# A gate whose bias is added by TensorE and whose logits are copied by ScalarE, in a language-model tower with attention and a mixture of experts

## What is computed

```
logits = jnp.einsum('btd,de->bte', x, Wg) + bg
gates = jax.nn.softmax(logits, axis=-1)
vals, idx = jax.lax.top_k(gates, TOP_K)
vals = vals / (jnp.sum(vals, axis=-1, keepdims=True) + EPS)
```

## Time and profile before

| | us |
|---|---|
| median of 3 runs | 352.75 |
| lowest and highest run | 352.64 and 353.0 |
| the profiled execution, its own time | 354.0 |
| its span, first to last instruction | 352.2 |
| mean granted TensorE clock | 0.973 |

### The profile page before, as it was taken

The page is one execution under the profiler, slowest core; times in us unless marked ns, Lnnn a source line. Parts: engine busy times, 40 slices in busy tenths (PEclk is TensorE's granted clock), DMA queues, the critical chain, the costliest instruction groups (busy, mean ns, idle before and its releaser), DMA issues.

```text
span 352.2 us, 11441 instructions
## 1 busy us (share of the span) xinstructions
PE 325.4 (92%) x3017; PEld 289.2 (82%) x3017; DVE 302.1 (86%) x1190; ACT 255.4 (73%) x754; POOL 197.3 (56%) x346
## 2 busy tenths in 40 slices
PE   8947999999999999999978699999998999999983
PEld 3615888888878787878867698999998999999972
DVE  6686999999989999999996487999986877778986
ACT  1636889999979898999975477776766776776730
POOL 7011320777775677767747367788875454554520
PEclk9986999999999999999998899999999999999999
DMA  6066760000000100000012022323333222226857
GB/s 168 19 183 167 217 227 2 28 34 27 29 27 34 36 29 25 25 25 34 34 35 76 19 69 73 87 85 86 107 120 92 77 68 78 73 75 204 249 174 243
DMA packets 33130, 30.46 MB, mean 86 GB/s; under 512 B 4701, under 2 KB 27320, under 8 KB 33080
## 3 DMA queue, kind: packets, MB, share of 16 engines
q1 hardware_dynamic: 25848, 18.81, 18.5%
q0 software_dynamic: 4224, 9.18, 7.6%
q10 hardware_dynamic: 3008, 1.89, 1.8%
HBM read 16.42 MB, written 13.44 MB: 85 GB/s over the span
## 4 chain that ended last, share of the span: by engine, by line
PE 45%; DVE 29%; issue 13%; DMA 4%; ACT 3%; DVEq 2%; SPq 2%; ACTq 0%
PE ps_oy L1818 6%; PE ps_out L1808 6%; PE ps_v L1818 6%; PE ps_q L1808 5%; DVE qk_max L1087 3%; DVE k_prime L1093 3%; DVE q_prime L1093 3%; PE ps_oy L1729 3%; PE ps_out L1713 3%; DVE stats L1070 2%; PE ps_qT L1701 2%; PE ps_qT L1800 2%; PE ps_k L1808 2%; DVE h L1082 1%; DVE heads_out L1105 1%
## 5 line engine op out<-in xcount | busy, mean ns | idle before, releaser
L777 POOL DMA_INDIRECT y_dram<-heads_out,place x68 | 69.4, 1021 | 45.9 <-ACT heads_out L969 36.5
L755 POOL DMA_INDIRECT slots_dram<-rows,row_id x64 | 64.6, 1010 | 20.4 <-issue 19.9
L960 ACT ACTIVATE k_prime<-ps_out,b_T 128x128 f32<-128x128 f32 x105 | 31.4, 366 | 19.0 <-PE ps_out L1808 18.7
L960 ACT ACTIVATE k_prime<-ps_q,b_T 128x128 f32<-128x128 f32 x108 | 31.9, 365 | 17.0 <-PE ps_q L1808 16.8
L1818 PE MATMUL ps_oy<-w_tile,k_prime 128*128 128x128 f32 x288 | 38.4, 276 | 1.4 <-issue 1.3
L1713 PE MATMUL ps_out<-context,qT 128*128 128x130 f32 x256 | 37.7, 291 | 0.0
L1818 PE MATMUL ps_v<-w_tile,k_prime 128*128 128x128 f32 x280 | 37.1, 276 | 0.5 <-issue 0.4
L1808 PE MATMUL ps_out<-sT,w_tile 128*128 128x128 f32 x280 | 37.1, 275 | 0.0
L1818 PEld LDWEIGHTS ps_oy<-w_tile,k_prime 128*128 128x128 f32 x288 | 35.0, 192 | 2.1 <-issue 2.1
L1729 PE MATMUL ps_oy<-out_w,oT 128*128 128x128 f32 x256 | 36.4, 286 | 0.0
L729 POOL TENSOR_TENSOR rstd<-moments,ln_eps 128x4 f32<-128x4 f32 (+1 forms) x19 | 3.7, 195 | 57.2 <-DVE moments L1076 56.6
(11 more groups left out here) (282 smaller groups left out, 865.2 us busy)
## 6 DMA issues: line engine op xcount, KB each, us to landing
qkv_rows<-slots_dram SPq DMA_DIRECT2D x71, 72.0 KB
y_sum<-y_dram SPq DMA_DIRECT2D x14, 256.0 KB, 3.4
w_all<-in_L_ffn_W SPq DMA_DIRECT2D x1, 2048.0 KB, 14.0
w_all<-in_L_ffn_W SPq DMA_DIRECT2D x8, 256.0 KB, 4.3
out<-h SPq DMA_DIRECT2D x6, 256.0 KB, 3.5
y_dram<-heads_out,place POOLq DMA_INDIRECT x68
y_dram<-y_sum SPq DMA_DIRECT2D x2, 512.0 KB, 5.6
slots_dram<-rows,row_id POOLq DMA_INDIRECT x64, 2.3
```

Source lines behind the costliest of these rows:

```text
L755: nc.gpsimd.indirect_dma_start(slots_dram[:, :], bass.IndirectOffsetOnAxis(row_id[:, place_of(p, a), j, k:k + 1], 0), rows[:, place_of(p, ...
L777: nc.gpsimd.indirect_dma_start(y_dram[:, :], bass.IndirectOffsetOnAxis(place[:, a, :], 0), y[:, a, :], None).then_inc(s_placed[a], 16)
L960: last = nc.scalar.activation(hT[:, a % 2, c, :], ps_up[a % 2][0][:, c * P:c * P + P], ACT.Relu, bias=b1_T[:, bass.ds(experts[0] * FC + c, ...
```

## The change

It touches one small step on five engines:

- PE: `gate_product` gets one more matmul ahead of its two. A row of 128 ones (one partition) is the stationary operand and the bias, repeated twice (16 numbers on one partition), the moving one, so that PSUM holds the bias before the two products are added to it.
- ACT: a new function `logits_copy`, which waits for `s_lg`, copies the 128 x 16 logits from PSUM to `logits` and releases `s_lgr`. It is called at the end of ACT's `sequence`, behind `qT_copy`.
- DVE: `read_logits` is no longer called in `odd`; the wait for `s_lgr` stays. For the last two sequences `gates` still reads the logits on DVE, by a plain copy.
- POOL sets one more small tile, `ones_row`, among the constants at the start.
- The bias is loaded once (1 x 8, 32 bytes) instead of to 128 partitions.

```diff
-        gate_b = sb("gate_b", [P, E])
+        gate_b = sb("gate_b", [1, E])
+        ones_row = sb("ones_row", [1, P])
...
+            nc.gpsimd.memset(ones_row[:, :], 1.0)
...
-            act.dma_start(gate_b[:, :], b_gate.rearrange("(o d) -> o d", o=1).to_broadcast([P, E])).then_inc(s_gate_w, 16)
+            act.dma_start(gate_b[:, :], b_gate.rearrange("(o d) -> o d", o=1)).then_inc(s_gate_w, 16)
...
+            def logits_copy(p):
+                act.wait_ge(s_lg, p + 1)
+                nc.scalar.activation(logits[:, :, :], ps_ln[:, 0:2 * E].rearrange("p (j e) -> p j e", j=2), ACT.Copy)\
+                    .then_inc(s_lgr, 1)
...
                 if live(t + 2, TILES):
                     k_exp(t + 2, 1 - a, 0)
                     qT_copy(t + 2, 0)
+                if live(p - 2):
+                    logits_copy(p - 2)
...
-            def read_logits(p):
+            def read_last_logits(p):
                 dve.wait_ge(s_lg, p + 1)
-                nc.vector.tensor_tensor(logits[:, :, :], ps_ln[:, 0:2 * E].rearrange("p (j e) -> p j e", j=2),
-                                        gate_b[:, None, :].to_broadcast([P, 2, E]), ALU.add).then_inc(s_lgr, 1)
-
+                nc.vector.tensor_copy(logits[:, :, :], ps_ln[:, 0:2 * E].rearrange("p (j e) -> p j e", j=2)).then_inc(s_lgr, 1)
...
                 if live(p - 2):
-                    read_logits(p - 2)
                     dve.wait_ge(s_lgr, p - 1)
...
+                nc.tensor.matmul(ps_ln[:, 0:2 * E].rearrange("p (j e) -> p j e", j=2), ones_row[:, :],
+                                 gate_b[:, None, :].to_broadcast([1, 2, E]), start=True, stop=False, skip_group_check=True)
                 for j in range(2):
                     last = nc.tensor.matmul(ps_ln[:, j * E:j * E + E], x2T[:, a, j * P:j * P + P], gate_w[:, :],
-                                            start=True, stop=True)
+                                            start=False, stop=(j == 1), skip_group_check=True)
                 last.then_inc(s_lg, 1)
```

More of the change, by code:

```diff
@@ L1278, in gates @@
             def gates(p):
-                read_logits(p)
+                read_last_logits(p)
                 dve.wait_ge(s_lgr, p + 1)
```

## The result

| | before | after |
|---|---|---|
| median of 4 runs, us | 352.88 | 358.1 |
| lowest and highest | 352.64 and 353.02 | 357.46 and 358.49 |
| span of the profiled execution | 352.2 | 356.6 |
| gates p = 2 to p = 14 | 121.73 | 126.65 |
| gate p = 14 to gate p = 15 | 12.23 | 10.83 |

The kernel is slower, by a ratio of 1.0147, 95% interval 1.0133 to 1.0161. Forecast were 355.1 us and a range of 352.0 to 357.4: the sign is right, the loss of 5.2 us is more than twice the 2.3 forecast, and the time lies outside the range.

A forecast was written before the change was run, and what follows sets the result against it. DVE was taken to bound the kernel, with a ring through ACT and PE closing behind the change. Gate steps, the last read and the expert stage summed to +2.3 us on 352.75, giving 355.1 us; range 352.0 to 357.4.

The forecast's parts named there:

- The ring closes: Gate, ACT's logits copy, q_exp and queue, PE's transposes, next gate: 10.05 us in straight code, 10.26 in the loop.
- The price b: On PE, two bias passes with a one-row stationary operand ahead of the gate: 0.22 us, ends 0.06 and 0.44.
- a first pass far from 0.11: Sign of being wrong, on PE: the first bias pass taking a time far from the assumed 0.11 us.
- The price L: On ACT, start of the logits copy to start of q_exp: 0.15 us in straight code, 0.25 in loop and edges.
- Rival 4: Dear copy (0.31 us) and bias (0.22) throughout: 356.3 us, near 359 with a bias of 0.44; chance 0.2.
- p = 2 to 6: Four gate periods in straight code, 39.27 us before, 40.20 forecast: +0.93.
- p = 7 to 9: Two gate periods, one with loop work and straight copy, 20.16 us before: +0.26.
- p = 9 to 13: Four gate periods in the hardware loop, 40.28 us before, 41.04 forecast: +0.76.
- p = 14 to 15: Where DVE makes slot lists and PE waits for its mask: residual 1.02 us behind the gate instead of 1.52, -0.50.
- Rival 3: TensorE's clock behind the mask wait of 1.96 us holds in one of two slices: 353.6 us; chance 0.08.
- Rival 2: Same closed ring, but cheap bias (0.06 us) and copy (0.10): 351.5 us, up to 352.5; chance 0.13.
- Rival 1: DVE's relief reaches the end in full, 3.5 us gained, gates 9.6 apart: 349.3 us; chance 0.07.

The follow-up runs named there:

- no_bias: The change with the addition of the gate's bias left out, the logits copy still on ScalarE; 350.04 us, 0.9895 of the kernel before.
- full_rows: The change with the bias and the row of ones on 128 partitions, zeros in the bias's others; 354.51 us, 1.0012 of the kernel before.
- first: The change with the logits copy moved to the start of the next sequence on ScalarE, before its first q_exp; 358.38 us, 1.0146 of the kernel before.
- dve_reads: The change with the one-row bias kept on TensorE, but VectorE copying the logits at its old read; 357.16 us, 1.0098 of the kernel before.
- parts: The change with the bias split into three bf16 parts, added by one bf16 product of 96 rows; 352.12 us, 0.9968 of the kernel before.

## Why the prediction was right in sign and short in size

- **The ring closes.** Right. Copy, q_exp, ACT's unbroken queue, transposes and gate follow each other as forecast; the 6.85, 0.77 and 1.51 were measured as 6.83, 0.77 and 1.60. But the closing alone doesn't give the sign: closed and without the bias (no_bias) the gates p = 2 to 14 took 1.25 less than before. With a bias at the price that was forecast (full_rows) they took 1.40 more, where 2.34 was forecast, and that time isn't clear of the kernel before (1.0012 [0.9978, 1.0045]). That the loss came out so clearly is owed to the term that failed: in that the sign owes something to luck.
- **The price b** is the term that failed. I took 2 x 0.11 = 0.22, "since type and columns are the gate's", with 0.44 as upper end. Measured: bias to context product 0.86 for 0.44, and 0.09 more between the transposes and the bias, 0.51 in all. full_rows with the same type, columns and repeated view has 9.96 - 9.74 = 0.22, so the term was right for 128 rows; what failed is that the number of rows was taken not to matter. Of the prediction's own signs of being wrong, a first pass far from 0.11 came true: the two passes take 0.32 to the gate's first product (68.23 to 68.55), in full_rows 0.14 (78.40 to 78.54). The Trainium skill, "TensorE: Matmul & The Clock Gate", section on LDWEIGHTS, has a load's time follow the columns alone. The loads here agree that the rows don't count (0.29 and 0.30 for two), though two take more than the 0.21 worked out by its figure. That says nothing of whether loads overlap their neighbours', and there 0.29 us was lost. From gate 2 to 14 it is 126.65 - 123.13 = 3.52 us, more than the whole miss (5.2 instead of 2.3 us).
- **The price L** was 0.08 in straight code, under the lower end of 0.10; q_exp overlaps the copy. Rival 4 names a budget for an ACTIVATE: the Trainium skill, "ScalarE: Activation LUTs", rules for kernel authors, gives about 0.3 us for one whose bias is a pointer operand. That isn't this copy, which names no bias, lasts 0.18 and has q_exp 0.08 behind it; an instruction with such a bias (L904) does last 0.30. In the loop I spread 0.25 over all gates "at its edges, where register work and the branch are no longer hidden". The place was right: it is 0.56 and 0.52 at the two turns, 0.27 and 0.21 where the loop is entered and left, and about 0.1 elsewhere. first shows that most of it belongs to the turn and can be hidden.
- **The steps.** p = 2 to 6 +1.72 (forecast +0.93); p = 6 to 7 +0.52 (+0.22); p = 7 to 9 +0.56 (+0.26); p = 9 to 13 +1.71 (+0.76); p = 13 to 14 +0.41 (+0.17); p = 14 to 15 -1.40 (-0.50); the read for p = 15 +0.42 (+0.28). The first gate stood 0.32 later, and the stage after took 0.14 longer (+0.22). Sum +4.4, as the spans have it. The straight period was 0.20 over the forecast: b +0.29, L -0.07, ACT's queue -0.02.
- **p = 14 to 15.** The residual came 185.81 - 184.63 = 1.18 behind the gate, where 1.02 was forecast and 1.52 stood before, and PE's wait fell by 0.36. Rival 3's clock came on top: 1.00 instead of 0.86. That it hid some 0.9 us of the loss is luck. In the fourteen profiles the distance is 10.5 to 11.3 in the seven with 1.00 there, and 11.7 to 12.5 in the seven with 0.85 or 0.86. Which a kernel gets isn't settled: the change and first both waited 1.60 for the mask, and got one each.
- **What was not seen: the second ring.** The prediction asked what DVE's relief would uncover and found one ring. The one through the context product, 9.67 in the kernel before, needs no copy on ScalarE. So the bias alone costs 2.97 (dve_reads), the copy alone gains 1.25 (no_bias), and both together cost 4.92: prices don't add where the longest of several rings counts.
- **The rivals.** Rival 4 had the mechanism with larger prices, 356.3 and with b = 0.44 near 359; the result lies between, from the bias and not from the copy. Rival 2's prices are nearly those of parts (b = 0.11), which took 352.12, beside 351.5 to 352.5 in its sum. Rival 1 needed slack on ACT, and there was none: even without the bias the gates stand 9.74 apart and not 9.6.

## What to carry to other kernels

When an instruction moves off the engine that sets the pace, list every ring through its new engine, those behind it in the queue included: here two stood within 0.1 us of the bound. Here a tiny matmul was priced by what it did to the loads around it, so look for a row of its own shape between such neighbours, and try it with the neighbours' row count or as one bf16 product. Where a hardware loop turns, put the instruction that waits behind the turn and not in front of it.

## What the runs showed of the hardware

- An fp32 product with a stationary operand of 1, 32 or 64 rows between products of 128 rows costs 0.51 us a gate, with 128 rows 0.22, and one bf16 product of 96 rows 0.11.
- The turn of the loop on ScalarE costs 0.45 us where nothing covers it, and 0.07 where it stands ahead of a wait.
- A granted clock of 1.00 instead of 0.86 between gates 14 and 15 goes with about 1.2 us (10.83 in the change, 12.02 in first).
